# First pointwise stage of a quantised block: seven tiles instead of eight evicted by Vector, the last one among them, and the halvings of the running maximum moved ahead of it

## The chip, the cores and the metric

The kernel runs on one core of a Trainium2 chip. TensorE multiplies matrices into PSUM, Scalar (ACT) and Vector (DVE) read PSUM and write SBUF, and every engine has its own instruction stream in program order. Engines wait for each other by semaphores. The metric is the device time of one execution in microseconds; lower is better.

## The reference

The input has 16 images of 32 channels and 32 x 32 pixels. A dense block of dilated convolutions with a two-dimensional cosine transform comes first, and then a quantised block of three convolutions. The change touches the first of the three, a pointwise convolution from 32 to 192 channels, and the scale that the second needs:

```python
def _fake_quant(x, bits):
    qmax = 2.0 ** (bits - 1) - 1.0
    scale = jnp.maximum(jnp.max(jnp.abs(x)) / qmax, 1e-08)
    y = x / scale
    yq = jnp.clip(y + jax.lax.stop_gradient(jnp.round(y) - y), -qmax - 1.0, qmax)
    return yq * scale
...
out = jax.nn.relu(_qconv(x, w1))
out = jax.nn.relu(_qconv(out, w2, stride=1, padding=1, groups=PLANES))
out = _qconv(out, w3)
return out + x
```

The quantisation of the second convolution's input needs the maximum over the whole output of the first. So nothing of the second can start before the last element of the first has gone into that maximum.

## The kernel before

The first 304 us are the dense block. Then `quantised_block` runs its three convolutions one after the other: c1 (pointwise), c2 (depthwise, as matmuls with diagonal weights) and c3 (pointwise), with a rescaling between them.

**Tiles of c1.** The output has 36 tiles (`C1_TILES`), each 128 partitions by 772 columns (two pieces of `CUT` = 386). Tile n lies in PSUM in the slot n % 4, two banks each, so four tiles fit in PSUM at a time: TensorE makes tile n only once tile n - 4 has been evicted (semaphores `c1_out` for Scalar's tiles, `c1_out_dve` for Vector's). A tile is two matmuls (L1349). The offset that quantisation asks for is added in one of two ways: tiles in `C1_OFFSET` get it by two more matmuls (L1332) and are evicted without a bias (L1080 on Scalar); the others get it as the bias of Scalar's eviction (L1082). All of Vector's tiles are in `C1_OFFSET`.

**Who evicts.** `C1_DVE` lists Vector's tiles (3, 7, 11, 16, 20, 25, 29, 32), `C1_ACT` is the rest (28 tiles). An eviction applies the ReLU and writes f16 to `I` (in c1 seen as `by_tile`). Vector's eviction (L1182) also leaves the tile's maximum in a column of `c1_peak`, by an accumulator that a second short instruction reads.

**The maximum of Scalar's tiles.** Scalar's tiles go in pairs (`C1_PAIRS`), and Vector folds each pair (2 x 772 columns) into the running maximum `c1_most` (L1168 the first time, L1172 afterwards). A fold waits for Scalar's tiles (`c1_out`) and for the fold before it (`c1_folded`). Ahead of its eviction of tile n, Vector folds the pairs whose second tile is below n - 2. At the end the last two Scalar tiles, which are in no pair, are folded one by one (L1189), the two halves of `c1_most` become one (L1193, 772 columns), that is halved again (L1194, 386 columns), reduced to one column (L1196), and with the columns of `c1_peak` reduced to one number for each partition (L1197). `link` marks steps that wait for the one before, by the semaphore `chain`.

**After it.** `rescale(1)` turns the number into a scale: TensorE transposes it (L1308), Vector reduces it (L1129), TensorE spreads it over the partitions (L1312), and Vector works out the factors (L1135 to L1140). Then Vector quantises (L1206) and c2 starts (L1387). `keep_busy` (L1318) puts matmuls whose result nobody reads into the stretches in which TensorE would wait.

Of the kernel before, what the change touches and what calls it, by code (L numbers as in the profile page):

```python
# [9 lines left out]
ALU = mybir.AluOpType  # L10
# [39 lines left out]
CUT = 386  # L50
# [954 lines left out]
def quantised_block(nc, block, semaphore, out, keep):  # L1005
# [7 lines left out]
    with ExitStack() as ctx:  # L1013
        def sb(name, shape, dt=F32):
            return ctx.enter_context(nc.sbuf_tensor("q_" + name, shape, dt))

        def sem(name):
            return semaphore("q_" + name)
# [9 lines left out]
        by_tile = I[:].rearrange("p g b (k n) -> p (g b k n)", n=CUT).rearrange("p (t n) -> p t n", n=2 * CUT)  # L1028
        x_cuts = xq[:].rearrange("p b (k n) -> p (b k) n", n=CUT)
        f_cuts = fields[:].rearrange("p b (k n) -> p (b k) n", n=CUT)  # L1030
        Iq = I[:].bitcast(BF16)
        c1_peak = sb("c1_peak", [NP, len(C1_DVE) + 1])
        c1_most = sb("c1_most", [NP, 2, 2 * CUT], F16)
# [7 lines left out]
        chain = sem("chain")  # L1041
# [4 lines left out]
        c1_folded, c2_folded = sem("c1_folded"), sem("c2_folded")  # L1046
        c2_last, c2_last_dve, c2_relu = sem("c2_last"), sem("c2_last_dve"), sem("c2_relu")
        c2_half = sem("c2_half")
        c1_done, c1_out, c1_out_dve = sem("c1_done"), sem("c1_out"), sem("c1_out_dve")
# [19 lines left out]
        def _(act):  # L1069
# [7 lines left out]
            for n in C1_ACT:  # L1077
                act.wait_ge(c1_done, n + 1)
                if n in C1_OFFSET:
                    nc.scalar.activation(c1_tile(by_tile, n), c1_slot(ps, n), ACT.Relu).then_inc(c1_out, 1)  # L1080
# [26 lines left out]
        def _(dve):  # L1107
# [3 lines left out]
            def link(ins):  # L1111

                done[0] += 1
                ins.then_inc(chain, 1)
                dve.wait_ge(chain, done[0])
# [48 lines left out]
            def fold_pair(i):  # L1164

                dve.wait_ge(c1_out, 2 * i + 2)
                if i == 1:
                    nc.vector.tensor_tensor(out=c1_most[:], in0=c1_pair(by_tile, 0), in1=c1_pair(by_tile, 1),  # L1168
                                            op=ALU.max).then_inc(c1_folded, 1)
                else:  # L1170
                    dve.wait_ge(c1_folded, i - 1)
                    nc.vector.tensor_tensor(out=c1_most[:], in0=c1_most[:], in1=c1_pair(by_tile, i),  # L1172
                                            op=ALU.max).then_inc(c1_folded, 1)

            since = 1
            for m, n in enumerate(C1_DVE):
                until = sum(pair[1] < n - 2 for pair in C1_PAIRS)
                for i in range(since, until):
                    fold_pair(i)
                since = max(since, until)  # L1180
                dve.wait_ge(c1_done, n + 1)
                nc.vector.tensor_scalar(c1_tile(by_tile, n), c1_slot(ps, n), 0.0, 0.0, ALU.max, ALU.max,  # L1182
                                        accum_out=c1_peak[:, m:m + 1]).then_inc(c1_out_dve, 1)
            for i in range(since, len(C1_PAIRS)):
                fold_pair(i)
            for n in range(2):
                dve.wait_ge(c1_out, len(C1_ACT) - 1 + n)
                dve.wait_ge(c1_folded, len(C1_PAIRS) - 1)
                nc.vector.tensor_tensor(out=c1_most[:, n], in0=c1_most[:, n],  # L1189
                                        in1=by_tile[:, C1_ACT[n - 2]], op=ALU.max).then_inc(c1_folded, 1)  # L1190
            dve.wait_ge(c1_out_dve, len(C1_DVE))
            dve.wait_ge(c1_folded, len(C1_PAIRS) + 1)
            link(nc.vector.tensor_tensor(out=c1_most[:, 0], in0=c1_most[:, 0], in1=c1_most[:, 1], op=ALU.max))  # L1193
            link(nc.vector.tensor_tensor(out=c1_most[:, 1, 0:CUT], in0=c1_most[:, 0, 0:CUT],  # L1194
                                         in1=c1_most[:, 0, CUT:2 * CUT], op=ALU.max))
            link(nc.vector.tensor_reduce(c1_peak[:, len(C1_DVE):], c1_most[:, 1, 0:CUT], AX.X, ALU.max))  # L1196
            nc.vector.tensor_reduce(stat[:, 1:2], c1_peak[:], AX.X, ALU.max).then_inc(stat_ready, 1)  # L1197
            rescale(1)
# [91 lines left out]
            for b in range(NB):  # L1290
# [3 lines left out]
                if b == 0:  # L1294
                    dve.wait_ge(scaled, 3)
                    nc.vector.tensor_tensor(out=last_scale[:], in0=sc[:, 2, 2:3], in1=keep.w_scale[:, 2:3],
                                            op=ALU.mult).then_inc(scale_read, 1)
# [6 lines left out]
        def _(pe):  # L1304
# [10 lines left out]
            def keep_busy(count, bank=5):  # L1315

                for _ in range(count):
                    nc.tensor.matmul(ps[:, bank], w_q[:, 0:NP], w_q[:, 0:HALF], start=True, stop=True)  # L1318
# [11 lines left out]
            def offset(n):  # L1330
                for h in range(2):
                    nc.tensor.matmul(c1_slot(ps, n)[:, h], w_q[:, NP * (n // 6):NP * (n // 6) + NP],  # L1332
                                     minus_zero[:, 0:CUT], start=True, stop=False, skip_group_check=True)
# [3 lines left out]
            for n in range(C1_TILES):  # L1337
                if n >= 4:
                    mine, out_by = (C1_DVE, c1_out_dve) if n - 4 in C1_DVE else (C1_ACT, c1_out)
                    pe.wait_ge(out_by, mine.index(n - 4) + 1)  # L1340
                if n < 6:
                    pe.wait_ge(xq_ready, (1, 2, 2, 3, 3, 3)[n])
                if n == 4:
                    pe.wait_ge(xq_act, 1)
                if n in C1_OFFSET and n not in C1_AHEAD:
                    offset(n)
                for h in range(2):
                    at = CUT * (2 * (n % 6) + h)
                    last = nc.tensor.matmul(c1_slot(ps, n)[:, h], w_q[:, NP * (n // 6):NP * (n // 6) + NP],  # L1349
                                            x_low[:, at:at + CUT], start=n not in C1_OFFSET, stop=True,  # L1350
                                            skip_group_check=True)
                last.then_inc(c1_done, 1)
            pe.wait_ge(c1_out_dve, len(C1_DVE))
            for last in range(2, -1, -1):
                pe.wait_ge(c1_out, len(C1_ACT) - last)
                keep_busy(2, 1)
            pe.wait_ge(c1_folded, len(C1_PAIRS) + 1)
            keep_busy(2)
            for links in range(LINKS + 1, LINKS + 4):
                pe.wait_ge(chain, links)  # L1360
                keep_busy(1)
            spread_stat(1, between=lambda: keep_busy(2))
# [51 lines left out]
            keep_busy(2, 4)  # L1414
            pe.wait_ge(chain, C2_LINKS)
            keep_busy(2, 4)
# [6 lines left out]
            for b in range(NB):  # L1423
# [3 lines left out]
                for n, (h, cols) in enumerate(c3_pieces(b)):  # L1427
# [5 lines left out]
                    for g in range(NG):  # L1433
                        if b == n == 0 and g == 2:
                            pe.wait_ge(q3_ready, 2)
                        if b == n == 0 and g == 5:
                            pe.wait_ge(q3_act, 1)
                        w3 = w3_swap[:, g] if b % 2 else w_q[:, W1 + NP * g:W1 + NP * g + NP]
                        last = nc.tensor.matmul(bank, w3,  # L1439
                                                Iq[:, g, b, HALF * h + cols.start:HALF * h + cols.stop], start=False,  # L1440
                                                stop=g == NG - 1, skip_group_check=True)
# [17 lines left out]

C2_TURNS = {4: 2, 8: 6, 10: 8}  # L1460
LINKS = 0
C2_LINKS = LINKS + 10
C1_TILES = 6 * NG
C1_DVE = [3, 7, 11, 16, 20, 25, 29, 32]
C1_ACT = [n for n in range(C1_TILES) if n not in C1_DVE]
C1_PAIRS = list(zip(C1_ACT[0:-2:2], C1_ACT[1:-2:2]))
C1_OFFSET = C1_DVE + [0, 1, 2, 5, 8, 10, 13, 15, 18, 21, 23, 26, 28, 31, 33, 35]
C1_AHEAD = [0, 1, 2]


# [11 lines left out]
def c1_slot(ps, n):  # L1482
    return ps[:, 2 * (n % 4):2 * (n % 4) + 2, 0:CUT]


def c1_tile(by_tile, n):
    return by_tile[:, n].rearrange("p (k i) -> p k i", k=2)


def c1_pair(by_tile, i):  # L1490
    a, b = C1_PAIRS[i]
    return by_tile[:, a:b + 1:b - a]
# [116 lines left out]
```

## Time and profile before

| | |
|---|---|
| three runs | 387.30, 387.79 and 390.51 us |
| median | 387.79 us |
| span of the profiled execution (first to last instruction) | 387.3 us; no other time of that execution is recorded |
| mean granted TensorE clock | 1.000 |
| busy share of the span: TensorE, Vector, Scalar | 96%, 74%, 61% |
| c1 and its maximum, until the first matmul of c2 | about 304 to 333.6 us |

The span is given to a tenth. Its 387.3 equals the lowest of the three runs, so a difference worked out in the trace is laid on the median of the runs. A time in the trace counts from the first instruction. Where an instruction waits for another, the profile shows the idle time before it and what ended it.

### The profile page before, as it was taken

The numbers are of one execution on the slowest core, as the hardware profiler recorded it, in microseconds if no ns is written. First come the engines' busy times: TensorE is split into PE (matmuls) and PEld (weight loads), VectorE is DVE, ScalarE is ACT, GpSimd is POOL, SyncE is SP. The second block draws the span as 40 slices with busy tenths as digits, with TensorE's granted clock in tenths as the row PEclk, the third lists the DMA queues.
The fourth block names the chain that finished last, engine by engine and source line by source line (L and its number), as shares of the span: only waits on it lengthen the run. The fifth ranks groups of instructions, "written<-read, shape, count | busy, mean of one in ns | idle before, by whom it ended". The sixth has DMA issues, their size and how long they took to land.

```text
span 387.3 us, 7803 instructions
## 1 busy us (share of the span) xinstructions
PE 371.7 (96%) x2891; PEld 268.5 (69%) x2891; DVE 286.2 (74%) x533; ACT 235.2 (61%) x380; POOL 13.5 (3%) x17
## 2 busy tenths in 40 slices
PE   8979999999999999899999999999989899999986
PEld 7757877888687868687876878687866354345533
DVE  5777677847956893689379648936897699777886
ACT  5436749555952775386459546842865698278771
POOL 6000000120030000000000000000000000000000
PEclk9999999999999999999999999999999999999999
DMA  7846335225442523362245315133400000000005
GB/s 232 252 103 183 75 92 172 61 50 118 131 95 55 141 84 80 82 151 67 61 113 149 87 42 126 50 86 82 108 2 3 0 1 2 0 4 2 2 27 193
DMA packets 19678, 32.57 MB, mean 84 GB/s; under 512 B 4544, under 2 KB 11840, under 8 KB 19648
## 3 DMA queue, kind: packets, MB, share of 16 engines
q1 hardware_dynamic: 19008, 31.14, 30.6%
q10 hardware_dynamic: 640, 1.03, 1.2%
q8 instruction: 19, 0.31, 0.3%
q14 instruction: 11, 0.09, 0.1%
HBM read 11.38 MB, written 2.10 MB: 35 GB/s over the span
## 4 chain that ended last, share of the span: by engine, by line
PE 77%; DVE 9%; DMA 5%; ACT 5%; issue 2%; SPq 1%; ACTq 0%; DVEq 0%
PE sums_ps L768 29%; PE mix_ps L871 13%; PE ps L1387 9%; PE mix_ps L900 5%; PE sums_ps L827 5%; PE mix_ps L827 5%; DMA D<-D 4%; PE mix_ps L875 4%; PE ps L1439 3%; ACT q_I L1080 2%; ACT q_I L1082 2%; PE mix_ps L909 2%; DVE part L499 1%; DMA w_raw<-in_w_conv 1%; DVE Zt L541 1%
## 5 line engine op out<-in xcount | busy, mean ns | idle before, releaser
L768 PE MATMUL sums_ps<-D,w_hl 128*128 128x512 f32 x504 | 122.9, 399 | 1.8 <-DMA D<-D 1.8
L768 PEld LDWEIGHTS sums_ps<-D,w_hl 128*128 128x128 f32 x504 | 93.4, 188 | 31.9 <-issue 6.4
L871 PE MATMUL mix_ps<-mix_hl,F_hl 128*128 128x288 f32 x360 | 64.4, 296 | 0.2 <-ACT Y L390 0.2
L390 ACT ACTIVATE Y<-mix_ps 128x288 f32<-128x288 f32 x120 | 48.9, 410 | 24.8 <-PE mix_ps L875 12.9
L871 PEld LDWEIGHTS mix_ps<-mix_hl,F_hl 128*128 128x128 f32 x360 | 55.4, 190 | 2.5 <-ACT Y L390 0.8
L328 ACT ACTIVATE r<-sums_ps,bias_sb 64x512 f32<-64x512 f32 x28 | 19.1, 682 | 47.6 <-PE sums_ps L768 47.4
L499 DVE TENSOR_TENSOR part<-mix_ps,part 64x512 f32<-64x512 f32 x16 | 11.1, 693 | 40.7 <-PE mix_ps L827 40.3
L875 PE MATMUL mix_ps<-mix_hl,X 96*128 96x288 f32 x120 | 35.2, 298 | 0.0
L1387 PE MATMUL ps<-q_q,diag 64*64 64x512 bf16 x576 | 33.4, 389 | 0.1
L348 ACT ACTIVATE D<-part 64x512 fp32r<-64x512 f32 x16 | 10.7, 671 | 33.3 <-DVE part L505 33.3
L1088 ACT ACTIVATE q_I<-ps,w_bias 128x1024 f32 x20 | 21.2, 1110 | 14.5 <-PE ps L1387 14.5
L1387 PEld LDWEIGHTS ps<-q_q,diag 64*64 64x64 bf16 x576 | 16.9, 105 | 16.6 <-PE ps L1387 1.5
L900 PE MATMUL mix_ps<-Y,hc 32*32 32x512 f32 (+1 forms) x576 | 24.4, 567 | 0.6 <-ACT Y L390 0.6
L827 PE MATMUL sums_ps<-D,w_hl 128*128 128x512 f32 x96 | 23.9, 397 | 0.8 <-DMA D<-D 0.8
L827 PE MATMUL mix_ps<-D,w_hl 128*128 128x512 f32 x96 | 23.8, 397 | 0.0
L481 DVE CAST D<-r 64x512 fp32r<-64x512 f32 x32 | 13.4, 420 | 14.0 <-ACT r L328 13.4
L564 DVE SCALAR_TENSOR_TENSOR values<-St,b_sb,xb 64x128 f32<-64x128 f32 (+1 forms) x64 | 22.2, 346 | 0.9
L483 DVE TENSOR_TENSOR D<-r,D 64x512 fp32r<-64x512 f32 x32 | 21.9, 685 | 1.1
L875 PEld LDWEIGHTS mix_ps<-mix_hl,X 96*128 96x128 f32 x120 | 22.4, 188 | 0.0
L531 DVE SCALAR_TENSOR_TENSOR X<-part,X 32x512 fp32r<-32x512 f32 x32 | 21.8, 680 | 0.7
L827 PEld LDWEIGHTS sums_ps<-D,w_hl 128*128 128x128 f32 x96 | 17.6, 189 | 4.8 <-DMA D<-D 1.2
L380 ACT ACTIVATE X<-part 32x512 fp32r<-32x512 f32 x32 | 20.1, 629 | 0.6
(145 smaller groups left out, 512.9 us busy)
## 6 DMA issues: line engine op xcount, KB each, us to landing
D<-D SPq DMA_DIRECT2D x88, 126.0 KB, 2.3
x_own<-in_x_pads SPq DMA_DIRECT2D x16, 288.0 KB, 3.4
F<-r SPq DMA_DIRECT2D x64, 64.0 KB, 2.0
F<-in_x_mix SPq DMA_DIRECT2D x16, 128.0 KB, 2.4
F<-part SPq DMA_DIRECT2D x32, 64.0 KB, 2.0
xb<-in_x_res SPq DMA_DIRECT2D x8, 256.0 KB, 2.7
out<-q_res SPq DMA_DIRECT2D x7, 256.0 KB, 2.0
w_raw<-in_w_conv SPq DMA_DIRECT2D x6, 192.0 KB, 4.3
```

The lines of the kernel that those rows point to most:

```text
L380: last = nc.scalar.activation(X4[u][64:96, h], part[u][k].rearrange("p a b l -> p (a b l)"), ACT.Relu)
L390: nc.scalar.activation(Y[:, u, g], banks(p, u)[:, g % 4, 0:MIX], ACT.Copy).then_inc(y_out, 1)
L483: nc.vector.tensor_tensor(out=own(f, u, 1), in0=src, in1=high.bitcast(F32), op=ALU.subtract).then_inc(own_ready[u], 1)
L531: last = nc.vector.scalar_tensor_tensor(out=X4[u][low, h], in0=part[u][k].rearrange("p a b l -> p (a b l)"), scalar=0.0, in1=X4[u][k, h].b ...
L564: last = nc.vector.scalar_tensor_tensor(out=keep.values[64 * pi:64 * pi + 64, batch, m, PH // 2 * a:PH // 2 * (a + 1), :], in0=st[k, pi], ...
L768: last = nc.tensor.matmul(conv_sums(s, u)[:, bank, :], w_hl[:, wp, n, d, :], D[f][u][:, xp, :, 4 * d:4 * d + RUN], start=start and d == 0 ...
L827: last = nc.tensor.matmul(side_sums(s, u, f), w_hl[:, w, n, d, :], D[f - 1][u][:, x, :, 4 * d:4 * d + RUN], start=d == 0 and w == 0, stop= ...
L871: nc.tensor.matmul(y, F_hl[u][:, xp, h, k], mix_hl[:, wp], start=n == 0, stop=False, skip_group_check=True)
L875: nc.tensor.matmul(banks(p, u)[:, g % 4, 0:MIX], X4[u][:, g // 4, NP * (g % 4):NP * (g % 4) + NP], mix4_hl[:], start=False, stop=True, ski ...
L900: last = nc.tensor.matmul(out[32 * dy:32 * dy + 32, j, 0:PX // 4 * len(us)], hc[k, d], y, start=d == 0, stop=d == 2, skip_group_check=True)
L1088: nc.scalar.activation(I[:, g, b, 0:PX], ps[:, 2 * b:2 * b + 2].rearrange("p k n -> p (k n)"), ACT.Relu, bias=keep.w2_bias[:, bass.ts(g, 1 ...
L1387: last = nc.tensor.matmul(ps[64 * col:64 * col + 64, 2 * (two + b) + h], diag[rows, g, at:at + 2].rearrange("p q c -> p (q c)"), field[:, ...
```

## The change

Vector's tiles become 3, 8, 13, 18, 23, 28 and 35, the last being the last tile of all. Scalar has 29, and all but its last (tile 34) go in pairs, so that there are 14 pairs and 13 folds instead of 13 and 12. Ahead of its last eviction Vector does all folds that are left, and the two halvings. Behind it come two maxima over 386 columns: the two halves of tile 34 against each other, and the result against the running maximum; then the reduction as before. `C1_OFFSET` has 16 Scalar tiles as before, at other places. TensorE's `keep_busy` calls wait for other events.

```diff
             for m, n in enumerate(C1_DVE):
                 until = sum(pair[1] < n - 2 for pair in C1_PAIRS)
+                if n == C1_TILES - 1:
+                    until = len(C1_PAIRS)
                 for i in range(since, until):
                     fold_pair(i)
                 since = max(since, until)
+                if n == C1_TILES - 1:
+                    dve.wait_ge(c1_folded, len(C1_PAIRS) - 1)
+                    link(nc.vector.tensor_tensor(out=c1_most[:, 0], in0=c1_most[:, 0], in1=c1_most[:, 1], op=ALU.max))
+                    link(nc.vector.tensor_tensor(out=c1_most[:, 1, 0:CUT], in0=c1_most[:, 0, 0:CUT],
+                                                 in1=c1_most[:, 0, CUT:2 * CUT], op=ALU.max))
                 dve.wait_ge(c1_done, n + 1)
...
-            for i in range(since, len(C1_PAIRS)):
-                fold_pair(i)
-            for n in range(2):
-                dve.wait_ge(c1_out, len(C1_ACT) - 1 + n)
-                dve.wait_ge(c1_folded, len(C1_PAIRS) - 1)
-                nc.vector.tensor_tensor(out=c1_most[:, n], in0=c1_most[:, n],
-                                        in1=by_tile[:, C1_ACT[n - 2]], op=ALU.max).then_inc(c1_folded, 1)
+            final = by_tile[:, C1_ACT[-1]]
+            dve.wait_ge(c1_out, len(C1_ACT))
+            link(nc.vector.tensor_tensor(out=c1_most[:, 0, 0:CUT], in0=final[:, 0:CUT], in1=final[:, CUT:2 * CUT],
+                                         op=ALU.max))
+            link(nc.vector.tensor_tensor(out=c1_most[:, 1, 0:CUT], in0=c1_most[:, 1, 0:CUT],
+                                         in1=c1_most[:, 0, 0:CUT], op=ALU.max))
             dve.wait_ge(c1_out_dve, len(C1_DVE))
-            dve.wait_ge(c1_folded, len(C1_PAIRS) + 1)
-            link(nc.vector.tensor_tensor(out=c1_most[:, 0], in0=c1_most[:, 0], in1=c1_most[:, 1], op=ALU.max))
-            link(nc.vector.tensor_tensor(out=c1_most[:, 1, 0:CUT], in0=c1_most[:, 0, 0:CUT],
-                                         in1=c1_most[:, 0, CUT:2 * CUT], op=ALU.max))
             link(nc.vector.tensor_reduce(c1_peak[:, len(C1_DVE):], c1_most[:, 1, 0:CUT], AX.X, ALU.max))
...
+            pe.wait_ge(c1_out, len(C1_ACT) - 1)
+            keep_busy(3, 1)
+            pe.wait_ge(chain, LINKS + 2)
+            keep_busy(3, 1)
             pe.wait_ge(c1_out_dve, len(C1_DVE))
-            for last in range(2, -1, -1):
-                pe.wait_ge(c1_out, len(C1_ACT) - last)
-                keep_busy(2, 1)
-            pe.wait_ge(c1_folded, len(C1_PAIRS) + 1)
-            keep_busy(2)
-            for links in range(LINKS + 1, LINKS + 4):
+            keep_busy(2, 1)
+            pe.wait_ge(c1_out, len(C1_ACT))
+            for links in range(LINKS + 3, C1_LINKS + 1):
                 pe.wait_ge(chain, links)
                 keep_busy(1)
...
-C2_LINKS = LINKS + 10
+C1_LINKS = LINKS + 5
+C2_LINKS = C1_LINKS + 7
 C1_TILES = 6 * NG
-C1_DVE = [3, 7, 11, 16, 20, 25, 29, 32]
+C1_DVE = [3, 8, 13, 18, 23, 28, 35]
 C1_ACT = [n for n in range(C1_TILES) if n not in C1_DVE]
-C1_PAIRS = list(zip(C1_ACT[0:-2:2], C1_ACT[1:-2:2]))
-C1_OFFSET = C1_DVE + [0, 1, 2, 5, 8, 10, 13, 15, 18, 21, 23, 26, 28, 31, 33, 35]
+C1_PAIRS = list(zip(C1_ACT[0:-1:2], C1_ACT[1:-1:2]))
+C1_OFFSET = C1_DVE + [0, 1, 2, 5, 7, 10, 12, 15, 17, 20, 22, 25, 27, 30, 32, 34]
```

Vector's list from its last evictions to the end of the maximum, before (`q_c_most` is `c1_most`, `q_c_peak` is `c1_peak`, `q_I` the evicted tiles; in brackets the semaphores that a row waits for):

```order
L1182 TENSOR_SCALAR q_I,q_c_peak<-ps 128x772 [waits q_c1_done]
L1172 TENSOR_TENSOR q_c_most<-q_c_most,q_I 128x1544 [waits q_c1_folded,q_c1_out] x2
L1189 TENSOR_TENSOR q_c_most<-q_c_most,q_I 128x772 [waits q_c1_folded,q_c1_out] x2
L1193 TENSOR_TENSOR q_c_most<-q_c_most 128x772 [waits q_c1_folded,q_c1_out_dve]
L1194 TENSOR_TENSOR q_c_most<-q_c_most 128x386 [waits q_chain]
L1196 TENSOR_REDUCE q_c_peak<-q_c_most 128x1 [waits q_chain]
```

And now, from the eviction of tile 28 on:

```order
L1189 TENSOR_SCALAR q_I,q_c_peak<-ps 128x772 [waits q_c1_done]
L1172 TENSOR_TENSOR q_c_most<-q_c_most,q_I 128x1544 [waits q_c1_folded,q_c1_out] x4
L1185 TENSOR_TENSOR q_c_most<-q_c_most 128x772 [waits q_c1_folded]
L1186 TENSOR_TENSOR q_c_most<-q_c_most 128x386 [waits q_chain]
L1189 TENSOR_SCALAR q_I,q_c_peak<-ps 128x772 [waits q_c1_done,q_chain]
L1193 TENSOR_TENSOR q_c_most<-q_I 128x386 [waits q_c1_out]
L1195 TENSOR_TENSOR q_c_most<-q_c_most 128x386 [waits q_chain]
L1198 TENSOR_REDUCE q_c_peak<-q_c_most 128x1 [waits q_c1_out_dve,q_chain]
```

Four folds now stand in a row between Vector's last two evictions, the halvings have moved in front of the last eviction, and two rows of 386 columns stand in the place of the two single tiles.

TensorE's list behind the last tile, before: the keep-busy matmuls and what each group waits for, up to the transpose.

```order
L1318 MATMUL ps<-w_q 128x512 [waits q_c1_out,q_c1_out_dve]
L1318 MATMUL ps<-w_q 128x512
L1318 MATMUL ps<-w_q 128x512 [waits q_c1_out]
L1318 MATMUL ps<-w_q 128x512
L1318 MATMUL ps<-w_q 128x512 [waits q_c1_out]
L1318 MATMUL ps<-w_q 128x512
L1318 MATMUL ps<-w_q 128x512 [waits q_c1_folded]
L1318 MATMUL ps<-w_q 128x512
L1318 MATMUL ps<-w_q 128x512 [waits q_chain] x3
L1308 MATMUL ps<-ident,q_stat 1x128 [waits q_stat_ready]
```

And now:

```order
L1320 MATMUL ps<-w_q 128x512 [waits q_c1_out]
L1320 MATMUL ps<-w_q 128x512 x2
L1320 MATMUL ps<-w_q 128x512 [waits q_chain]
L1320 MATMUL ps<-w_q 128x512 x2
L1320 MATMUL ps<-w_q 128x512 [waits q_c1_out_dve]
L1320 MATMUL ps<-w_q 128x512
L1320 MATMUL ps<-w_q 128x512 [waits q_chain,q_c1_out]
L1320 MATMUL ps<-w_q 128x512 [waits q_chain] x2
L1310 MATMUL ps<-ident,q_stat 1x128 [waits q_stat_ready]
```

There are eleven before and eleven now; the first three now wait for Scalar's tile 33, the next three for the second halving, and the next two for Vector's last tile.

## Rows read from the trace of the kernel before

**Rows 1.** Windows: start:end, length, busy us (instructions) by engine, clock, DMA share, GB/s

```profile
304.00:328.00 24.00, 23.07 (x133) 11.43 (x130) 21.11 (x35) 23.62 (x32) 0.00 (x0) 1.00 0.00 1
328.00:332.00 4.00, 3.10 (x12) 0.87 (x12) 3.10 (x9) 0.09 (x1) 0.00 (x0) 1.00 0.00 0
```

**Rows 2.** The chain of waits in order of time: start, length, engine and line

```profile
309.04 0.79 ACT q_I L1082
309.83 0.70 ACT q_I L1080
...
321.02 0.80 ACT q_I L1082
...
321.87 0.50 PE ps L1332 x2
322.37 0.34 PE ps L1349 x2
...
323.04 0.36 PE ps L1349 x2
...
323.42 0.04 DVE q_I L1182
...
327.13 0.97 DVE q_c_most L1172
...
328.19 0.06 DVE q_c_most L1189
```

**Rows 3.** Scalar in order of time: start, length, line, shapes, idle time before

```profile
308.92 0.91 ACT L1082 ACTIVATE q_I<-ps,q_w_bias 128x772 f16<-128x772 f32 x1
...
324.57 0.94 ACT L1080 ACTIVATE q_I<-ps 128x772 f16<-128x772 f32 x1
325.78 0.81 ACT L1080 ACTIVATE q_I<-ps 128x772 f16<-128x772 f32 x1 [0.27 <-PE ps L1349]
...
327.28 0.81 ACT L1080 ACTIVATE q_I<-ps 128x772 f16<-128x772 f32 x1
336.86 1.11 ACT L1088 ACTIVATE q_I<-ps,w_bias 128x1024 f32 x1 [8.77 <-PE ps L1387]
```

**Rows 4.** Vector in order of time

```profile
309.87 0.96 DVE L1168 TENSOR_TENSOR q_c_most<-q_I 128x1544 f16<-128x1544 f16 x1 [0.44 <-ACT q_I L1082]
...
325.19 0.95 DVE L1182 TENSOR_SCALAR_CACHE_REDUCE q_I<-ps 128x772 f16<-128x772 f32 x1
326.07 0.08 DVE L1182 DVE_READ_ACCUMULATOR q_I<-ps 128x1 f32 x1
...
329.33 0.56 DVE L1193 TENSOR_TENSOR q_c_most<-q_c_most 128x772 f16<-128x772 f16 x1
329.93 0.36 DVE L1194 TENSOR_TENSOR q_c_most<-q_c_most 128x386 f16<-128x386 f16 x1
330.32 0.55 DVE L1196 TENSOR_REDUCE q_c_peak<-q_c_most 128x1 f32<-128x386 f16 x1
330.91 0.16 DVE L1197 TENSOR_REDUCE q_stat<-q_c_peak 128x1 f32<-128x9 f32 x1
```

**Rows 5.** TensorE in order of time, an early piece and the end of c1

```profile
26.70 0.50 PE L768 MATMUL mix_ps<-D,w_hl 128*128 128x512 f32 x1 [1.88 <-DMA D<-D]
...
329.28 1.45 PE L1318 MATMUL ps<-w_q 128*128 128x512 bf16 x4 [0.53 <-DVE q_c_most L1189]
...
332.76 0.82 PE L1318 MATMUL ps<-w_q 128*128 128x512 bf16 x3 [0.51 <-DVE q_sc L1137]
333.64 0.65 PE L1387 MATMUL ps<-q_q,diag 64*64 64x512 bf16 x8
```

**Rows 6.** The window around the early piece, columns as in the first group

```profile
24.00:28.00 4.00, 2.12 (x10) 1.39 (x9) 2.65 (x7) 1.36 (x2) 0.00 (x0) 1.00 0.20 50
```

**Rows 7.** Scalar in the depthwise stage, in order of time

```profile
339.62 2.12 ACT L1088 ACTIVATE q_I<-ps,w_bias 128x1024 f32 x2 [0.63 <-PE ps L1387]
342.38 1.11 ACT L1088 ACTIVATE q_I<-ps,w_bias 128x1024 f32 x1 [0.65 <-PE ps L1387]
```

## The prediction

> **What bounds the kernel now.** I read the page first: one core, a span of 387.3 us, and a chain of waits that is matmul work for most of its length. All edits of the change lie in the first pointwise stage, 304 to 333 us of the span, so I read that stage alone, by windows and then by the chain of waits in order of time.
>
> The windows [rows 1] show Scalar busy for 23.62 of the 24 us from 304 to 328, Vector for 21.11, and then four microseconds (328 to 332) in which Scalar does nothing and Vector closes the maximum. Nothing else can run there: the next stage needs the scale that this maximum gives. TensorE's granted clock is 1.00 in both, the upper level, 2.4 GHz.
>
> The chain [rows 2] says what ends last. From 309.04 to 321.82 it is Scalar alone, eviction after eviction, 0.79 for one with a bias (L1082) and 0.70 for one without (L1080). At 321.82 tile 24 comes out; TensorE then makes tiles 28 and 29 in 1.58 (321.82 to 323.40), and from 323.42 to 330.91 the chain is Vector: evict 29, fold, evict 32, two folds, two single tiles, two halvings, the reduction. So the stage is limited by Scalar for its length and by Vector at its end. Scalar's last eviction starts at 327.28 and takes 0.81, so it is out at 328.09 [rows 3], while Vector's last fold, begun at 327.13, lets the first single go at 328.19 [rows 2]: both engines end together, and 2.8 us of Vector work follow.
>
> **The change part by part.**
>
> *One tile more on Scalar.* Up to tile 24 both kernels give Scalar 20 tiles, nine with a bias and eight without after the first three. So tile 24 is out at 321.82 in both. After it the changed Scalar has 25, 26, 27, 29, 30, 31, 32, 33, 34, without a bias and with one in turn. Four pairs end with tile 33: 321.82 + 4 x (0.70 + 0.79) = 327.78; tile 34 is out 0.70 later, at 328.48, only 0.39 after the old last tile, because the old list lost time near its end: between the starts at 324.57 and 325.78 lie 1.21 where 0.69 to 0.79 is usual [rows 3], with 0.27 of plain idleness, waiting for TensorE. I assume that no such stall comes in the new list. Where one could come is tile 32, whose place Vector's tile 28 must free. TensorE has 28 ready at 322.71 (two offset and two main matmuls, 321.87 to 322.37 + 0.34 [rows 2]), Vector takes 0.96 for it (0.88 until the read of the accumulator at 326.07, and 0.08 for that [rows 4]), so it is out at about 323.7, and tile 32, which has an offset too, needs the same 0.84 of TensorE. Scalar wants it at 327.78 - 0.79 - 0.70 = 326.29. Slack about 1.7, so I cost it at nothing, with 0 to 1 as bounds.
>
> Beside this price stands one of the Trainium skill. ScalarE: Activation LUTs, section "What ACT_TABLE_LOAD costs", gives 186 + 0.833 N ns without a pointer operand, 93 more with one, and 93 of overlap back to back. For 772 columns that is an estimate of 0.736 and 0.829, against the 0.70 and 0.79 of the rows; the four pairs would take 6.26 and not 5.96, and the sum below would be 0.3 higher. The rows measure this very instruction, so they decide.
>
> *Vector's list.* One eviction fewer, one pair fold more (13 instead of 12, since 28 tiles go in pairs instead of 26), the two single folds gone. The halvings move ahead of the last eviction, and two maxima of 386 columns are added behind it. What counts is what stands behind a tile of Scalar's. Before, behind tile 35 (328.09): one single, two halvings, the reduction, to 330.91. After, the last pair is (32, 33), and behind tile 33 Vector still has in this order: fold, halving of 772, halving of 386, eviction of 35, 386 columns of tile 34, 386 columns against the running maximum, reduction. Each has a row with the same shape and the same kind of wait on the one before:
> - fold of a pair until the next that waits for it: 327.13 to 328.19, 1.06 [rows 2];
> - halving of 772 columns: 329.33 to 329.93, 0.60; of 386: 329.93 to 330.32, 0.39; reduction: 330.32 to 330.91, 0.59 [rows 4];
> - eviction until Vector's next instruction: 325.19 to 326.07, 0.88 [rows 4];
> - the two new maxima, both of 386 columns: 0.39 each, as the second halving, whose shape and type they have. The upper bound is 0.60, the row of 772 columns; the lower 0.29, if they pay nothing for waiting on the one before (a fold takes 0.96 by itself and 1.06 to one that waits for it: 0.10 less).
>
> Sum: 1.06 + 0.60 + 0.39 + 0.88 + 0.39 + 0.39 + 0.59 = 4.30. A fold follows the Scalar eviction that it waits for by 0.04 (the Scalar eviction that began at 308.92 took 0.91, to 309.83; the fold begins at 309.87 [rows 3, 4]). So the maximum goes to the last small reduction at 327.78 + 0.04 + 4.30 = 332.12 instead of 330.91: **+1.21**. Fold 13 is not held up by the fold before it: its pair (30, 31) is out at 326.29, and 1.06 later is 327.39.
>
> In words: the change takes 0.88 from Vector, but puts a whole eviction and a fold between the last pair and the end, where before there was a half-width fold.
>
> *Cover.* Scalar is idle for 8.77 us after its last eviction [rows 3] and has no other work, so nothing hides the 1.21. The rescaling that follows, L1126 to L1140, is unchanged, and so are both later stages, which start from it. So 1.21 goes through to the end.
>
> *TensorE's tail.* The keep-busy matmuls are 11 before and 11 after, in other groups. One still stands behind the last link of the chain, as before, so the transpose is not delayed: nothing. What changes is the gap. After the three behind tile 33 (from about 327.8, some 0.8 long, as three in 0.82 at 332.76 [rows 5]) the next three wait for the second halving, which ends at 332.12 - 0.59 - 0.39 - 0.39 - 0.88 = 329.87: an idle stretch of about 1.2, where before the longest in this tail was 0.53 [rows 5]. In an early stretch of the same trace TensorE idled 1.88 [rows 5], and the window around it reads a clock of 1.00 [rows 6], so I cost this at nothing; the upper bound is the third rival.
>
> The profile's span of 387.30 is the lowest of the three runs, and the median is 387.79, so the sum is laid on the median: 387.79 + 1.21 = **389.0** (a span of about 388.5).
>
> **The rivals.**
>
> *Vector's own work decides* (Scalar's tiles come soon enough). Vector would then run without a gap from 322.73, where tile 28 is ready: 0.88, four folds of 1.06, and 0.60 + 0.39 + 0.88 + 0.39 + 0.39 + 0.59 = 3.24, together 8.36, to 331.09: +0.2, so 388.0. For it speaks that Vector's chain ends the stage today; against it, that it asks for tile 33 at 326.79, a microsecond before Scalar's pace has it. Even so the change gains nothing.
>
> *A gain: Scalar's pace rises when Vector reads PSUM less often.* Then tile 33 would have to be out at 326.57 just to be level. That is 1.21 off the 5.96 that four pairs take. Against it: Scalar's evictions are 0.70 and 0.79 with one alternation from 309 to 321 [rows 2], whether Vector evicts or folds at the time. It would give 387 at best.
>
> *Slower by more than 1%: the clock falls.* The place is the 1.2 us idle stretch before the second halving, the price what the depthwise stage pays at the lower level, 1.2 GHz. A pair of batches there takes 2.76 (339.62 to 342.38 [rows 7]); at half the clock one pair costs 2.76 more and two 5.5. It decides from one pair on, since 1.21 + 2.76 = 3.97 is 1% of the time; two pairs give 387.79 + 1.21 + 5.5 = 394.5. No row of this stage shows the lower level.
>
> *Scalar starves at tile 32.* Should Vector be late with tile 28 by more than the 1.7 of slack, each microsecond beyond goes straight on tile 33 and the end; with 1 us 390.0.
>
> **How the numbers follow.** Forecast 389.0, chance 0.76. Vector's own work, 388.0: 0.12. A gain, 387: 0.04. Starving, 390.0: 0.04. The clock, 394.5: 0.04. The price of the added maxima moves the forecast by -0.2 to +0.4, and single runs of the same kernel lie 3 us apart (387.30 to 390.51), so the range is 387.2 to 390.6: it holds the forecast with its bounds, the first rival and the fourth, and some of that spread. About 1% (3.9 us) is what a measurement of this kernel can tell from no change; below 383.9 I see nothing but an accident, 0.02; above 391.7 stand the clock and a share of the unknown, 0.05; within 0.93. I expect a small loss that will hardly show in the times and plainly in the trace.
>
> **What would show it.** Scalar's evictions should run from 306.8 to about 328.5 with no break, 29 of them. Vector's fold of the last pair should begin right after tile 33 near 327.8, and there should be idle time on Vector ahead of the last two folds, ended by Scalar. From that fold to the small reduction: 4.3. The first depthwise matmul should come 1.2 later than 333.64 [rows 5]. The prediction is wrong if tile 33 is out before 327, if the eviction of tile 35 slips ahead of the last fold, or if the granted clock of the depthwise stage is below 1.00.

## The result, and the profile after

The changed kernel takes 389.29 us (median of 22 runs, 388.10 to 391.29) against 387.89 (22 runs, 386.62 to 390.51). The ratio is 1.0033, with a 95% interval from 1.0019 to 1.0048: 1.3 us slower, between 0.7 and 1.9. That is clear of noise and well below 1%.

The spans of the two profiled executions hide it: 387.3 before, 387.4 after. The profiled execution of the changed kernel has a time of its own, 389.25, so 1.85 us lie outside its span. In every run on record that has both numbers it is 1.73 to 1.86, so the profiled execution of before was not the run of 387.30 that shares its number. The dense block, which the change does not touch, ended later in the profiled execution of before: Scalar's first eviction of c1 begins at 306.84 there and at 305.61 here. So the stage is compared from that point.

The chain of waits of the changed kernel, in order of time (start, length, engine and line), answers to [rows 2] and [rows 4]:

```profile
307.81 0.80 ACT q_I L1082
...
325.10 0.70 ACT q_I L1080
325.81 0.80 ACT q_I L1082
326.61 0.02 issue
326.63 0.97 DVE q_c_most L1172
327.61 0.02 issue
327.63 0.57 DVE q_c_most L1185
328.20 0.02 issue
328.23 0.37 DVE q_c_most L1186
328.60 0.02 issue
328.62 0.97 DVE q_I L1189 x2
329.59 0.29 DVE q_c_most L1193
329.88 0.02 issue
329.90 0.37 DVE q_c_most L1195
330.27 0.02 issue
330.30 0.57 DVE q_c_peak L1198
```

Before, the chain left Scalar at tile 24, went through TensorE and then stayed on Vector for seven and a half microseconds. Now it is Scalar without a break from its first eviction to tile 33 at 326.61, and Vector only from there. The third eviction is out at 307.81, the small reduction begins at 330.89: 23.08 us, against 21.87 before (309.04 to 330.91 [rows 2, 4]). The difference is 1.21.

Vector in order of time, around its last folds:

```profile
322.65 2.02 DVE L1172 TENSOR_TENSOR q_c_most<-q_c_most,q_I 128x1544 f16<-128x1544 f16 x2
325.13 0.96 DVE L1172 TENSOR_TENSOR q_c_most<-q_c_most,q_I 128x1544 f16<-128x1544 f16 x1 [0.46 <-ACT q_I L1082]
326.63 0.96 DVE L1172 TENSOR_TENSOR q_c_most<-q_c_most,q_I 128x1544 f16<-128x1544 f16 x1 [0.54 <-ACT q_I L1082]
...
330.89 0.16 DVE L1199 TENSOR_REDUCE q_stat<-q_c_peak 128x1 f32<-128x8 f32 x1
```

Vector now waits for Scalar twice, 0.46 and 0.54, with a whole eviction still ahead of it. Then Scalar and TensorE, in the rows that answer to [rows 3] and [rows 5]:

```profile
326.25 1.06 ACT L1080 ACTIVATE q_I<-ps 128x772 f16<-128x772 f32 x1
336.84 2.12 ACT L1088 ACTIVATE q_I<-ps,w_bias 128x1024 f32 x2 [9.53 <-PE ps L1390]
```

```profile
326.65 0.82 PE L1320 MATMUL ps<-w_q 128*128 128x512 bf16 x3 [0.65 <-ACT q_I L1082]
328.64 0.82 PE L1320 MATMUL ps<-w_q 128*128 128x512 bf16 x3 [1.17 <-DVE q_c_most L1186]
...
333.62 6.73 PE L1390 MATMUL ps<-q_q,diag 64*64 64x512 bf16 x112
```

Scalar sits idle 9.53 us and not 8.77. TensorE's new gap is 1.17 long. From Scalar's first eviction to the first depthwise matmul it is 333.62 - 305.61 = 28.01, against 333.64 - 306.84 = 26.80: again 1.21. The window from 328 to 332 still reads a granted clock of 1.00, as in [rows 1]:

```profile
328.00:332.00 4.00, 2.96 (x13) 1.00 (x13) 3.22 (x10) 0.00 (x0) 0.00 (x0) 1.00 0.00 0
```

### The profile page after: what moved, and what is told of

Same layout as the page of the kernel before. It is cut to its first block, busy times and chain, and to the rows that moved or that the text cites. A ratio compares the mean times of both kernels' runs of the same rounds, so it can differ in the third digit from the quotient of the medians.

```text
span 387.4 us, 7799 instructions
## 1 busy us (share of the span) xinstructions
PE 371.7 (96%) x2889; PEld 269.4 (70%) x2889; DVE 286.2 (74%) x532; ACT 236.3 (61%) x381; POOL 13.5 (3%) x17
## 4 chain that ended last, share of the span: by engine, by line
PE 77%; DVE 9%; ACT 7%; DMA 4%; issue 2%; DVEq 0%; ACTq 0%
PE sums_ps L768 28%; PE mix_ps L871 13%; PE ps L1390 9%; PE mix_ps L900 5%; PE mix_ps L827 5%; PE sums_ps L827 5%; PE mix_ps L875 4%; DMA D<-D 4%; ACT q_I L1080 3%; ACT q_I L1082 3%; PE ps L1442 3%; DVE part L499 2%; PE mix_ps L909 1%; PE mix_ps L811 1%; PE mix_ps L768 1%
## 5 line engine op out<-in xcount | busy, mean ns | idle before, releaser
L768 PEld LDWEIGHTS sums_ps<-D,w_hl 128*128 128x128 f32 x504 | 93.4, 188 | 32.4 <-issue 6.3
L1390 PEld LDWEIGHTS ps<-q_q,diag 64*64 64x64 bf16 x576 | 18.0, 105 | 15.6 <-issue 1.3
L522 DVE SCALAR_TENSOR_TENSOR F_hl<-F,F_hl 128x1024 fp32r<-128x1024 f32 x16 | 19.5, 1217 | 2.1 <-ACT F_hl L364 1.8
```

Source lines behind the costliest of these rows:

```text
L768: last = nc.tensor.matmul(conv_sums(s, u)[:, bank, :], w_hl[:, wp, n, d, :], D[f][u][:, xp, :, 4 * d:4 * d + RUN], start=start and d == 0 ...
L1390: last = nc.tensor.matmul(ps[64 * col:64 * col + 64, 2 * (two + b) + h], diag[rows, g, at:at + 2].rearrange("p q c -> p (q c)"), field[:, ...
```

## The experiments

"The stage" is the time from the start of Scalar's first eviction to the small reduction: 306.84 to 330.91 before, 24.07; 305.61 to 330.89 in the changed kernel, 25.28. Differences of half a microsecond are 0.13% of the time, less than an interval of these runs, so the stage in the trace carries the verdicts, and the ratios are given beside it. All ratios are against the kernel before. Each stage is read from one execution; how well it repeats can be seen once, since the run without keep-busy matmuls leaves Scalar's and Vector's work in this stage as it is: 25.24 against 25.28.

**Eviction of tile 35 ahead of the last fold.** On the changed kernel:

```diff
                 if n == C1_TILES - 1:
-                    until = len(C1_PAIRS)
+                    until = len(C1_PAIRS) - 1
...
-                if n == C1_TILES - 1:
-                    dve.wait_ge(c1_folded, len(C1_PAIRS) - 1)
-                    link(...)
-                    link(...)
                 dve.wait_ge(c1_done, n + 1)
...
+            fold_pair(len(C1_PAIRS) - 1)
+            dve.wait_ge(c1_folded, len(C1_PAIRS) - 1)
+            link(...)
+            link(...)
             final = by_tile[:, C1_ACT[-1]]
```

> The changed kernel, but Vector evicts tile 35 ahead of the fold of the last pair, not behind it; the halvings follow that fold. I measure the stage from the start of Scalar's first eviction to the small reduction at its end: 24.07 us in the kernel before, 25.28 in the changed one. Theory (a whole eviction behind the last pair is what costs): Vector idles 0.54 before the last fold, and tile 35 is ready about then, so the eviction fills this hole and the stage is 24.6 to 24.8, the time 0.5 to 0.6 below the changed kernel. Rival (the 29th Scalar tile is what costs): the stage stays at 25.2 to 25.3.

Measured: 388.69 us, ratio 1.0029 (1.0008 to 1.0050). Scalar's first eviction begins at 305.35, so the stage is 330.01 - 305.35 = 24.66. Vector's rows at the end:

```profile
324.85 0.96 DVE L1172 TENSOR_TENSOR q_c_most<-q_c_most,q_I 128x1544 f16<-128x1544 f16 x1 [0.45 <-ACT q_I L1082]
325.76 0.96 DVE L1184 TENSOR_SCALAR_CACHE_REDUCE q_I<-ps 128x772 f16<-128x772 f32 x1
326.65 0.08 DVE L1184 DVE_READ_ACCUMULATOR q_I<-ps 128x1 f32 x1
326.65 0.96 DVE L1172 TENSOR_TENSOR q_c_most<-q_c_most,q_I 128x1544 f16<-128x1544 f16 x1
...
330.01 0.16 DVE L1199 TENSOR_REDUCE q_stat<-q_c_peak 128x1 f32<-128x8 f32 x1
```

The idle time ahead of the last fold is gone, the eviction stands in it, and 0.62 of the 1.21 is back with the same 29 tiles on Scalar. To the first depthwise matmul the gain is 0.49 (332.87 - 305.35 = 27.52, against 28.01): eight keep-busy matmuls now come in a row behind the second halving, and the transpose waits for the last of them (Vector idles 0.53 for it, where it was 0.40). In the times this half microsecond can't be told from the changed kernel.

**Halvings behind the eviction.** On the changed kernel, the same three lines (the wait and the two links) moved from ahead of the eviction of tile 35 to ahead of `final`:

```diff
                 if n == C1_TILES - 1:
                     until = len(C1_PAIRS)
...
-                if n == C1_TILES - 1:
-                    dve.wait_ge(c1_folded, len(C1_PAIRS) - 1)
-                    link(...)
-                    link(...)
                 dve.wait_ge(c1_done, n + 1)
...
+            dve.wait_ge(c1_folded, len(C1_PAIRS) - 1)
+            link(...)
+            link(...)
             final = by_tile[:, C1_ACT[-1]]
```

> The changed kernel, but the two halvings stand behind the eviction of tile 35, not ahead of it. Theory (all of it is one chain on Vector, and the place of the halvings in it is worth nothing): the stage is 25.2 to 25.4, as in the changed kernel. Rival (doing the halvings early takes them out of the end): the stage is up to 0.99 longer, 26.2.

Measured: 388.94 us, ratio 1.0042 (1.0014 to 1.0069); the stage is 331.28 - 306.15 = 25.13. It is not longer, and 0.07 under the range that I gave: the eviction does not wait for the fold and starts 0.88 behind it (327.15 to 328.03), where the halving starts 1.00 behind it. To the first depthwise matmul it is 334.14 - 306.15 = 27.99, level with the changed kernel. So halving ahead of the eviction gives nothing: both stand in one chain on Vector.

**Seven tiles, the last of them 33.** On the changed kernel. The last eviction now comes ahead of the folds of the last two pairs, and the halvings behind all folds; of the edit only the lists are shown:

```diff
-C1_DVE = [3, 8, 13, 18, 23, 28, 35]
+C1_DVE = [3, 8, 13, 18, 23, 28, 33]
...
-C1_OFFSET = C1_DVE + [0, 1, 2, 5, 7, 10, 12, 15, 17, 20, 22, 25, 27, 30, 32, 34]
+C1_OFFSET = C1_DVE + [0, 1, 2, 5, 7, 10, 12, 15, 17, 20, 22, 25, 27, 30, 32, 35]
```

> The changed kernel with seven Vector tiles, but the last of them is tile 33 and Scalar takes 34 and 35; the halvings follow the last fold, and the last Scalar tile, 35, gets the two maxima of 386 columns. Theory (the place of the last eviction costs, not the count of seven): the eviction falls into Vector's idle time before the folds of the last two pairs, and behind the last pair stand only 1.00 + 0.60 + 0.39 + 0.39 + 0.40 + 0.59 = 3.37, so the stage is 24.3 to 24.5, 0.3 above the kernel before. Rival (one tile more on Scalar costs the 1.2): 25.2.

Measured: 388.40 us, ratio 1.0017 (0.9995 to 1.0040); the stage is 329.86 - 305.39 = 24.47. Vector's rows:

```profile
322.43 2.03 DVE L1172 TENSOR_TENSOR q_c_most<-q_c_most,q_I 128x1544 f16<-128x1544 f16 x2
324.54 0.96 DVE L1182 TENSOR_SCALAR_CACHE_REDUCE q_I<-ps 128x772 f16<-128x772 f32 x1
325.43 0.08 DVE L1182 DVE_READ_ACCUMULATOR q_I<-ps 128x1 f32 x1
325.43 2.03 DVE L1172 TENSOR_TENSOR q_c_most<-q_c_most,q_I 128x1544 f16<-128x1544 f16 x2
327.49 0.56 DVE L1187 TENSOR_TENSOR q_c_most<-q_c_most 128x772 f16<-128x772 f16 x1
```

The eviction at 324.54 fills both holes. The last eviction at tile 33 and not 35 makes the stage 0.81 shorter than in the changed kernel, or 0.66 against the run above, which has the halvings behind the folds as well; to the first depthwise matmul (332.72 - 305.39 = 27.33) it is 0.68 and 0.66.

The 0.40 that is left against the kernel before (24.47 against 24.07; 0.53 to the first depthwise matmul) is not the count of tiles alone, since this kernel also has the changed kernel's pairs and the changed end of the maximum. The kernel with eight tiles and every Scalar tile in a pair (the last one below) is the nearer comparison: there the last fold begins 21.09 behind Scalar's first eviction, and here 21.10 (at 326.49 by the chain of waits). From there to the small reduction it is 3.37 here and 2.65 there. The two maxima that the 29th Scalar tile brings (0.40 and 0.39) make up this difference but for 0.07.

**Eight tiles, the last of them 35.** On the kernel before:

```diff
-C1_DVE = [3, 7, 11, 16, 20, 25, 29, 32]
+C1_DVE = [3, 7, 11, 16, 20, 25, 29, 35]
...
-C1_OFFSET = C1_DVE + [0, 1, 2, 5, 8, 10, 13, 15, 18, 21, 23, 26, 28, 31, 33, 35]
+C1_OFFSET = C1_DVE + [0, 1, 2, 5, 8, 10, 13, 15, 18, 21, 23, 26, 28, 31, 33, 34]
```

> The kernel before, with eight Vector tiles and its own tail, but the last of the eight is tile 35 and not 32. Theory (before, both engines end together, and one Vector eviction moved by three tiles lands in the same full list): the stage is 24.0 to 24.3, no more than 0.2 from the kernel before. Rival (an eviction of the very last tile costs of itself, whatever the count): 24.9 to 25.0.

Measured: 387.52 us, ratio 0.9993 (0.9972 to 1.0013); the stage is 329.24 - 305.14 = 24.10. Vector's rows:

```profile
322.64 3.09 DVE L1172 TENSOR_TENSOR q_c_most<-q_c_most,q_I 128x1544 f16<-128x1544 f16 x3
325.65 0.95 DVE L1182 TENSOR_SCALAR_CACHE_REDUCE q_I<-ps 128x772 f16<-128x772 f32 x1
326.53 0.08 DVE L1182 DVE_READ_ACCUMULATOR q_I<-ps 128x1 f32 x1
326.53 1.02 DVE L1189 TENSOR_TENSOR q_c_most<-q_c_most,q_I 128x772 f16<-128x772 f16 x2
```

Three folds, the eviction and the singles follow one another with no idle time. An eviction of the very last tile costs nothing where Vector has work up to it and the rest of the maximum comes behind. This kernel keeps the old end of the maximum, so its last eviction stands ahead of the two single tiles; it differs from the changed kernel in this as well as in the count.

**No keep-busy matmuls.** On the changed kernel:

```diff
-            pe.wait_ge(c1_out, len(C1_ACT) - 1)
-            keep_busy(3, 1)
-            pe.wait_ge(chain, LINKS + 2)
-            keep_busy(3, 1)
             pe.wait_ge(c1_out_dve, len(C1_DVE))
-            keep_busy(2, 1)
             pe.wait_ge(c1_out, len(C1_ACT))
-            for links in range(LINKS + 3, C1_LINKS + 1):
-                pe.wait_ge(chain, links)
-                keep_busy(1)
+            pe.wait_ge(chain, C1_LINKS)
```

> The changed kernel without the eleven keep-busy matmuls between the last tile and the transpose; nothing else differs. TensorE then idles from the last tile to the transpose, about 5 us and not 1.2 at most. This prices the rival of the clock. Theory (an idle stretch of 1.2 leaves the clock alone, one of 5 does not): the granted clock of the depthwise stage falls below 1.00 for some microseconds, and the time rises by 2 to 6 us above the changed kernel. Rival (the keep-busy matmuls protect nothing): clock 1.00 throughout, the time within 0.5 us of the changed kernel. The stage itself, from Scalar's first eviction to the small reduction, is 25.2 to 25.4 in both.

Measured: 392.13 us, ratio 1.0110 (1.0077 to 1.0142); the stage is 330.69 - 305.45 = 25.24. TensorE's row at the end of the idle stretch, Scalar's first of the depthwise stage, and then the windows (start:end, length, busy time by engine, granted clock, DMA share, GB/s):

```profile
331.00 0.37 PE L1310 MATMUL ps<-ident,q_stat 128*1 128x128 f32 x1 [5.19 <-DVE q_sc L1126]
...
339.76 2.12 ACT L1088 ACTIVATE q_I<-ps,w_bias 128x1024 f32 x2 [12.64 <-PE ps L1383]
```

```profile
328.00:332.00 4.00, 1.00 (x3) 0.28 (x3) 3.03 (x10) 0.00 (x0) 0.00 (x0) 0.60 0.00 0
332.00:336.00 4.00, 3.49 (x22) 1.46 (x25) 3.15 (x12) 0.00 (x0) 0.00 (x0) 0.50 0.00 0
336.00:340.00 4.00, 4.00 (x52) 1.76 (x48) 1.24 (x3) 0.24 (x1) 0.00 (x0) 0.62 0.00 0
340.00:344.00 4.00, 4.00 (x76) 1.92 (x68) 1.39 (x2) 3.05 (x4) 0.00 (x0) 1.00 0.03 6
```

Behind 5.19 us of idle TensorE the clock falls to 0.50, the lower of the two levels (1.2 GHz), and it is back at 1.00 only in the window from 340. From Scalar's first eviction of c1 to its first of the depthwise stage it is 339.76 - 305.45 = 34.31, against 336.84 - 305.61 = 31.23: the lower level costs 3.1, and by the ratios, of four runs here, 3.0 (1.0110 against 1.0033). So the third rival's mechanism is real, and its price is near that of one pair of batches (2.76), not of two. In the changed kernel it did not occur: behind the idle 1.17 the clock stays at 1.00. In the run with the halvings behind the eviction TensorE idles 1.92 at this place, and the windows from 328 to 344 read 1.00 there too.

**Eight tiles, every Scalar tile in a pair.** Built from what the trace says, on the kernel before:

```diff
-            for n in range(2):
-                dve.wait_ge(c1_out, len(C1_ACT) - 1 + n)
-                dve.wait_ge(c1_folded, len(C1_PAIRS) - 1)
-                nc.vector.tensor_tensor(out=c1_most[:, n], in0=c1_most[:, n],
-                                        in1=by_tile[:, C1_ACT[n - 2]], op=ALU.max).then_inc(c1_folded, 1)
...
-C1_DVE = [3, 7, 11, 16, 20, 25, 29, 32]
+C1_DVE = [3, 7, 11, 16, 19, 24, 29, 33]
...
-C1_PAIRS = list(zip(C1_ACT[0:-2:2], C1_ACT[1:-2:2]))
-C1_OFFSET = C1_DVE + [0, 1, 2, 5, 8, 10, 13, 15, 18, 21, 23, 26, 28, 31, 33, 35]
+C1_PAIRS = list(zip(C1_ACT[0::2], C1_ACT[1::2]))
+C1_OFFSET = C1_DVE + [0, 1, 2, 5, 8, 10, 13, 15, 18, 21, 23, 26, 28, 31, 34]
```

(The waits for `c1_folded` count 13 folds accordingly.)

> A version built from the theory, on the kernel before: eight Vector tiles (3, 7, 11, 16, 19, 24, 29, 33), all 28 Scalar tiles in pairs, so that the last two go in one fold of 1.0 and not in two of 0.48 and 0.66; offsets by matmul alternate on Scalar's tiles to the end. Theory (Scalar's last tile and what stands behind it set the stage): Scalar loses none of the 0.47 that it lost in the kernel before and is out about 0.4 earlier, and behind it stand 1.0 + 0.60 + 0.39 + 0.59; the stage is 23.5 to 23.8 and the time 0.3 to 0.5 us below the kernel before. Rival (Vector's list is full, and an order with the same work gains nothing): 24.0 to 24.2.

Measured: 387.42 us, ratio 1.0004 (0.9982 to 1.0026); the stage is 329.59 - 305.85 = 23.74. Vector's rows:

```profile
325.00 0.95 DVE L1182 TENSOR_SCALAR_CACHE_REDUCE q_I<-ps 128x772 f16<-128x772 f32 x1
325.88 0.08 DVE L1182 DVE_READ_ACCUMULATOR q_I<-ps 128x1 f32 x1
325.88 2.02 DVE L1172 TENSOR_TENSOR q_c_most<-q_c_most,q_I 128x1544 f16<-128x1544 f16 x2
328.01 0.56 DVE L1188 TENSOR_TENSOR q_c_most<-q_c_most 128x772 f16<-128x772 f16 x1
329.59 0.16 DVE L1192 TENSOR_REDUCE q_stat<-q_c_peak 128x1 f32<-128x9 f32 x1
```

Vector's list runs on from the eviction at 325.00 through both folds to the halving at 328.01 without idle time. The stage is 0.33 shorter than before, within what was expected, and 0.33 is also what the first depthwise matmul gains (332.32 - 305.85 = 26.47 against 26.80). The way there is not quite the one expected. Scalar's last eviction (325.73, 1.11 long) is out at 326.84, 20.99 behind its first, against 21.25 before: 0.26 earlier and not 0.4. The last fold follows at 326.94 by the chain of waits, which stays on Vector there:

```profile
326.94 0.97 DVE q_c_most L1172
```

So the two engines still end together, and this fold is held by the fold before it and not by Scalar. In the time the gain does not show: the interval holds no change as well as a gain of 0.7 us. The version is inconclusive as a faster one; in the trace its stage is shorter by as much as the theory said.

## Why the prediction was right

**Scalar's pace.** The sum took 18.74 from the third eviction to tile 33 (309.04 to 327.78), four pairs of 1.49 behind tile 24 included. Measured: 307.81 to 326.61, 18.80. No stall came at tile 32: the assumption of slack held.

**Vector's end.** Predicted 4.30 from the last fold to the small reduction, measured 326.63 to 330.89, 4.26. Term by term: fold to halving 1.00 (I took 1.06, the spacing of two folds), halvings 0.60 and 0.39, eviction 0.89, the two new maxima 0.39 and 0.40, the reduction 0.59. The wait between Scalar's eviction and the fold was 0.02 and not 0.04. Errors of 0.06 in Scalar's pace and -0.06 here cancel. That the 1.21 is met to the last digit is luck; that it is met to within 0.1 is not, since no term was off by more than 0.06.

**What hides it.** Nothing did, as argued: 1.21 at the small reduction is 1.21 at the first depthwise matmul, from there to the end of the span both kernels take about the same (387.3 - 333.64 = 53.7 and 387.4 - 333.62 = 53.8), and in the runs it is 1.3 (0.7 to 1.9). Laying the sum on the median was right; the ground I gave for it, that the span of 387.3 is the lowest run, was not, since 1.85 us lie outside the span of the execution profiled after.

**The mechanism.** I had named a whole eviction and a fold between the last pair and the end. The experiments bear this out and divide it. With the eviction moved ahead of the last fold, 0.62 of the 1.21 comes back; with it at tile 33, ahead of the last two folds, 0.81 comes back (0.68 at the first depthwise matmul). The order of halvings and eviction is worth 0.15 in the stage and 0.02 at the first depthwise matmul. What is left is 0.40 in the stage (0.53 at the first depthwise matmul). Against the kernel with eight tiles and all pairs it is 0.73, and there it goes with the 29th Scalar tile, whose two maxima stand at the end and take 0.79. This last part is read from the rows of two kernels that differ in more than one thing, so it is argued and not shown.

What I had not seen is that, as far as these runs go, the place of the last eviction costs only where Vector has idle time ahead of it. With eight tiles the very last place costs 0.03, and Vector has no idle time from its eviction of tile 29 to the end; with seven it idles 0.46 and 0.54, and what it could have done in that time is what stands at the end. Whether the full list or the place ahead of the two single tiles makes it free with eight tiles is not separated.

**The rivals.** Vector's own work did not decide: it idled a microsecond ahead of its last two folds. Scalar's pace did not rise: the pairs take 1.50 in both kernels. The clock's fall is real: it came behind 5.19 us of idle TensorE and cost 3.1 us, and it did not come behind 1.17 us of it.

## What to carry to other kernels

Where two engines share a row of tiles and one of them also closes the reduction, look at what stands behind the other's last tile, not at the sum of work: moving a tile away from the engine that ends the stage made the stage longer, and half of the loss or more came from putting an eviction that stayed behind the last wait. Work that does not depend on the late tiles belongs in the idle time ahead of them. And compare a stage from its own first instruction: here two spans agreed to 0.1 us while the stage had moved by 1.2.

## What the runs showed of the hardware that was not expected

The dense block, the same in all these kernels, takes between 305.14 and 306.84 us up to Scalar's first eviction of c1, more than the change itself moves. A part of this seems to lie in TensorE's waits for the copies of the halos (`D<-D`) near 22 to 27 us: two waits in the kernel before (0.43, and the 1.88 of [rows 5]), one of 1.37 in the changed kernel, one of 0.68 with seven tiles and 33 last. TensorE's rows of these two:

```profile
22.58 4.47 PE L768 MATMUL mix_ps<-D,w_hl 128*128 128x512 f32 x18 [1.37 <-DMA D<-D]
```

```profile
22.06 4.44 PE L768 MATMUL mix_ps<-D,w_hl 128*128 128x512 f32 x18 [0.68 <-DMA D<-D]
```

The change leaves the instructions there as they are, so the difference lies between one execution and the next. These waits do not account for all of it: the kernel with eight tiles and 35 last waits 1.43 there and yet reaches Scalar's first eviction earliest (305.14), while the one that waits 0.68 reaches it at 305.39. Why they vary stays open.
